# Second expert layer of a two-layer decoder: ScalarE zeroes the accumulator, VectorE ends a tile ahead of the next bias, and batch 0 is normalised in the stage ahead

## The reference, cut to what matters

```python
x = hidden_states.reshape(-1, H)                       # 1024 tokens, H = 256
expert_idx = argmax(softmax(x @ Wr.T), -1)             # 8 experts
inter = zeros((1024, 1024))
for e in range(8):
    mask = (expert_idx == e)[:, None]
    inter = inter + mask * gelu(x @ W1[e] + b1[e])     # W1[e]: 256 x 1024
y = inter @ Wo + bo + x
out = (y - mean) * rsqrt(var + 1e-12) * gamma + beta   # added to the stream by the caller
```

## Time and profile before

| what | us |
| --- | --- |
| median of 3 runs (lowest, highest) | 1063.65 (1060.42, 1067.02) |
| the profiled execution, device time | 1065.01 |
| its span, first to last instruction | 1063.2 |
| second expert stage in the span | 914.4 to 1063.2 |
| PE busy over the span | 916.1 (86%) |
| DVE, ACT, POOL busy | 649.7 (61%), 461.4 (43%), 329.7 (31%) |
| mean granted TensorE clock | 0.937 |

### The profile page before, as it was taken

The page is one execution under the profiler, slowest core; times in us unless marked ns, Lnnn a source line. Parts: engine busy times, 40 slices in busy tenths (PEclk is TensorE's granted clock), DMA queues, the critical chain, the costliest instruction groups (busy, mean ns, idle before and its releaser), DMA issues. The chain is left out here.

```text
span 1063.2 us, 12776 instructions
## 1 busy us (share of the span) xinstructions
PE 916.1 (86%) x4044; PEld 465.7 (44%) x4044; DVE 649.7 (61%) x1329; ACT 461.4 (43%) x918; POOL 329.7 (31%) x336
## 2 busy tenths in 40 slices
PE   5878878999999964999799999997779997559975
PEld 2435534333332234567455555553323333434554
DVE  5856558888889534454165556544679994446443
ACT  3786444777777721121243333322128774013320
POOL 7226535200000001464074555541300000335514
PEclk9989999999999995999899999998979999659998
DMA  4040053033228208232930000001100100463000
GB/s 145 1 149 0 1 102 57 1 46 46 48 62 254 94 1 305 78 119 88 356 131 1 1 1 1 0 1 53 33 1 30 33 1 1 155 235 92 11 10 30
DMA packets 41653, 73.77 MB, mean 69 GB/s; under 512 B 8964, under 2 KB 27780, under 8 KB 40436
## 3 DMA queue, kind: packets, MB, share of 16 engines
q1 hardware_dynamic: 36228, 59.42, 18.6%
q0 software_dynamic: 4400, 13.11, 3.8%
q10 hardware_dynamic: 960, 0.43, 0.2%
HBM read 49.67 MB, written 10.49 MB: 57 GB/s over the span
## 5 line engine op out<-in xcount | busy, mean ns | idle before, releaser
L1063 DVE TENSOR_REDUCE c_amx<-PS 128x1 f32<-128x512 f32 x256 | 158.7, 682 | 29.8 <-PE PS L963 29.6
L1155 ACT ACTIVATE c_aE<-PS 128x512 f32<-128x512 f32 x256 | 132.5, 603 | 47.1 <-PE PS L975 46.9
L1764 POOL TENSOR_SCALAR s_Pn<-s_Pr,s_rs 128x512 f32<-128x512 f32 x64 | 99.9, 1563 | 108.2 <-DVE s_rs L1790 108.1
L68 POOL TENSOR_SCALAR rstd<-mv 128x4 f32<-128x4 f32 x8 | 1.9, 233 | 342.0 <-DVE mv L91 342.0
L963 PE MATMUL PS<-c_aKs,c_aQs 99*128 99x512 bf16 x256 | 95.1, 383 | 7.4 <-DMA c_aQs<-area 3.9
L975 PE MATMUL PS<-c_aQs,c_aKs 99*128 99x512 bf16 x256 | 94.5, 380 | 3.5 <-ACT c_aE L1155 2.3
L1848 ACT ACTIVATE s_Pr<-PS,s_nmx 128x512 f32<-128x512 f32 x64 | 44.0, 688 | 116.2 <-DVE s_nmx L1783 116.2
L1781 DVE TENSOR_REDUCE s_mx<-PS 128x1 f32<-128x512 f32 x64 | 44.2, 690 | 69.0 <-PE PS L1895 69.0
L1063 DVE TENSOR_REDUCE h_amx<-PS 128x1 f32<-128x512 f32 x128 | 79.7, 682 | 7.8 <-PE PS L963 7.5
L1155 ACT ACTIVATE h_aE<-PS 128x512 f32<-128x512 f32 x128 | 67.9, 601 | 23.6 <-PE PS L975 23.2
L986 PE MATMUL PS<-c_aE,c_VB 128*17 128x512 f32 x512 | 67.4, 598 | 0.1
(11 more groups left out here) (426 smaller groups left out, 1731.7 us busy)
## 6 DMA issues: line engine op xcount, KB each, us to landing
area<-in_e_w SPq DMA_DIRECT2D x16, 512.0 KB, 9.1
area<-in_g_w SPq DMA_DIRECT2D x8, 1024.0 KB, 15.9
c_aKs<-area SPq DMA_DIRECT2D x48, 128.0 KB
g_B<-in_g_b SPq DMA_DIRECT2D x1, 4096.0 KB, 15.8
c_aQs<-area SPq DMA_DIRECT2D x48, 64.0 KB
h_aQs<-h_QP SPq DMA_DIRECT2D x48, 64.0 KB
early<-in_ctxT SPq DMA_DIRECT2D x2, 1024.0 KB, 8.8
e_B<-in_e_b SPq DMA_DIRECT2D x1, 2048.0 KB, 11.4
```

The source lines that it names most:

```text
L1063: dve.tensor_reduce(self.mx[:, qt, j, half:half + 1], PS[:, n % MB, :], AX.X, ALU.max).then_inc(self.max_done, 1)
L1155: act.activation(self.E[kt % 2][:, j, :], PS[:, MB + x % XB, :], ACT.Exp, scale=0.25).then_inc(self.exp_done, 1)
L1764: pool.tensor_scalar(Pn[g % NPB][:, :], Pr[g % NPB][:, :], rs[:, g % NPB:g % NPB + 1], None, ALU.mult).then_inc(pn_ready, 1)
```

## The change

- `OutputProjection.vector` normalises the 4 tiles of batch 0 in its second call (b = 1), between the copies to XT and the additions of batch 1, after a wait for the first `rstd`. `normalise_vector`, `Norm` and `transposes_tensor` take a `first` and leave batch 0 out. This holds for both cross stages, so both expert stages begin with batch 1 alone, and TensorE transposes batch 0 with no wait.
- The router's matmuls wait for XT by batch. `SlotInverse.vector` makes V ahead of R, and the second expert stage reads the sources ahead of three more operations.
- In the second expert stage ScalarE zeroes `Hall`, by 8 activations with scale 0 that read the identity matrix. SyncE's transfers are in another order, under one semaphore each for what waits for them: the normalised rows first, then B1, the rows for the residual, W2, gamma and beta, B2.
- VectorE's loop runs `hidden(p+1)`, `add_hidden(p)` for p = 0 to 9. Then it waits for `rest_ready` and for each tile runs `add_hidden`, `residual(t)`, `finish(t)`, `hidden`. GpSimd scatters tile t right after its deviation. `down(7)` writes bank 0, and doesn't wait for `residual(6)`.
- The last stage doesn't clear its semaphores (`release` in place of `clear`).

```diff
+        if b == 1:
+            dve.wait_ge(self.following.rstd_ready, 1)
+            for i in range(TB):
+                dve.tensor_scalar(sh.XN[:, i, :], sh.X[:, i, :], sh.mv[:, i, 0:1], sh.rstd[:, i:i + 1],
+                                  ALU.subtract, ALU.mult).then_inc(self.first_normed, 1)
...
             self.following.tile(dve, i, self.out_taken, i + 1)
+        if b == 1:
+            dve.wait_ge(self.first_normed, TB)
...
+        c.link(dve.tensor_tensor(self.TH[:, :, :], self.tile1[:, :].unsqueeze(2).to_broadcast(wide),
+                                 self.iota.unsqueeze(1).to_broadcast(wide), ALU.is_equal))
+        dve.tensor_scalar(self.V[:, :, 0, :], self.TH[:, :, :], self.rowid, None, ALU.mult).then_inc(self.V_ready, 1)
+        dve.tensor_tensor(self.V[:, :, 1, :], self.TH[:, :, :], self.next_tile.unsqueeze(2).to_broadcast(wide),
+                          ALU.mult).then_inc(self.V_ready, 1)
...
             for i in range(NT):
+                pe.wait_ge(nm.xT_ready, KD * (i // TB + 1))
...
-            for d, s in ((wr, "g_wr"), (iota, "iota")):
-                sp.dma_start(d[tuple(slice(None) for _ in d.shape)], A[s]).then_inc(small_in, 16)
+            sp.dma_start(wr[:, :, :], A["g_wr"]).then_inc(wr_in, 16)
             sp.dma_start(inv.const[:, :], A["inv_const"]).then_inc(const_in, 16)
+            sp.dma_start(iota[:, :], A["iota"]).then_inc(iota_in, 16)
+            for b in range(B):
+                i = slice(b * TB, (b + 1) * TB)
+                nm.stored(sp, b)
+                sp.dma_start(xn_rows.rearrange("(t p) c -> p t c", p=P)[:, i, :], XN[:, i, :]).then_inc(xn_stored, 16)
+            sp.dma_start(B1[:, :], A["g_b1"].to_broadcast([P, EXP * F])).then_inc(b1_in, 16)
             whole = rows.rearrange("(t p) c -> p t c", p=P)
             sp.dma_start(whole[:, :, D:2 * D], X[:, :, :]).then_inc(rows_stored, 16)
-            for b in range(B):
-                i = slice(b * TB, (b + 1) * TB)
-                sp.wait_ge(nm.xn_ready, b + 1)
-                sp.dma_start(xn_rows.rearrange("(t p) c -> p t c", p=P)[:, i, :], XN[:, i, :]).then_inc(xn_stored, 16)
             sp.dma_start(whole[:, :, 0:D], XN[:, :, :]).then_inc(rows_stored, 16)
-            sp.dma_start(B1[:, :], A["g_b1"].to_broadcast([P, EXP * F])).then_inc(b_in, 16)
-            sp.dma_start(B2[:, :], A["g_b2"]).then_inc(b_in, 16)
             sp.dma_start(W2[:, :, :], A["g_w2"]).then_inc(w2_in, 16)
+            sp.dma_start(gb[:, :, :], A["g_gb"]).then_inc(rest_in, 16)
+            sp.dma_start(B2[:, :], A["g_b2"]).then_inc(rest_in, 16)
...
-            for i in range(NT):
-                last = pool.memset(Hall[:, i * F:(i + 1) * F], 0.0)
-            last.then_inc(hall_zero, 1)
...
                 inverse_deviation(t)
-                if t > 0:
-                    put_out(t - 1)
-            put_out(NT - 1)
+                put_out(t)
...
+            inv.vector_sources(dve, c)
             c.link(dve.tensor_tensor(turn[:, :], turn[:, :], iota[:, 0:EXP], ALU.add))
             c.link(dve.tensor_tensor(passed[:, :, 0:EXP - 1],
                                      turn[:, 0:EXP - 1].unsqueeze(1).to_broadcast([P, 16, EXP - 1]),
                                      iota[:, :].unsqueeze(2).to_broadcast([P, 16, EXP - 1]), ALU.is_lt))
             c.link(dve.tensor_reduce(exf[:, :], passed[:, :, 0:EXP - 1], AX.X, ALU.add))
-            inv.vector_sources(dve, c)
...
             hidden(0)
-            for p in range(NT + LAG + 2):
+            dve.wait_ge(hall_zero, NT)
+            for p in range(LAG + 1):
+                hidden(p + 1)
+                add_hidden(p)
+            dve.wait_ge(rest_in, 32)
+            dve.wait_ge(rest_ready, 1)
+            for t in range(NT):
+                p = LAG + 1 + t
+                if p < PAIRS:
+                    add_hidden(p)
+                residual(t)
+                finish(t)
                 if p + 1 < PAIRS:
                     hidden(p + 1)
-                if p == 0:
-                    dve.wait_ge(hall_zero, 1)
-                if p < PAIRS:
-                    add_hidden(p)
-                t = p - LAG - 1
-                if t == 0:
-                    dve.wait_ge(rest_ready, 1)
-                if 0 <= t < NT:
-                    residual(t)
-                if 0 <= t - 1 < NT:
-                    finish(t - 1)
...
+            for i in range(NT):
+                act.activation(Hall[:, i * F:(i + 1) * F].rearrange("p (k n) -> p k n", k=KF),
+                               sh.ident[:, :].unsqueeze(1).to_broadcast([P, KF, P]), ACT.Copy,
+                               scale=0.0).then_inc(hall_zero, 1)
...
             def down(t):
                 pe.wait_ge(hT_ready, t + 1)
-                if t > 0:
+                if 0 < t < NT - 1:
                     pe.wait_ge(z_ready, t)
+                elif t == NT - 1:
+                    pe.wait_ge(xsT_ready, PAIRS)
                 else:
                     pe.wait_ge(ids_ready, 1)
+                    pe.wait_ge(w2_in, 16)
                 for k in range(KF):
-                    last = pe.matmul(PS[:, 7, 0:D], HT[t % 2][:, k, :], W2[:, k, :],
+                    last = pe.matmul(PS[:, down_bank(t), 0:D], HT[t % 2][:, k, :], W2[:, k, :],
                                      start=(k == 0), stop=(k == KF - 1))
                 last.then_inc(w2_mm, 1)
 
             transpose_x(0)
...
             s(nc, own := StageSemaphores(nc), sh, A)
-            own.clear()
+            if n + 1 < len(stages):
+                own.clear()
+            else:
+                own.release()
```

More of the change, by code:

```diff
@@ L49, in layernorm_vector, with normalise_vector @@
     normalise_vector(dve, src, dst, mv, rstd, rstd_ready, normed)
-def normalise_vector(dve, src, dst, mv, rstd, rstd_ready, normed):
-    for b in range(B):
+def normalise_vector(dve, src, dst, mv, rstd, rstd_ready, normed, first=0):
+    for b in range(first, B):
         if rstd_ready is not None:
@@ L96, in gpsimd, with transposes_tensor @@
                                   self.var_ready, self.eps_added, self.rstd_ready)
-def transposes_tensor(pe, PS, XN, ident, ready, per_batch, done, loaded=None):
+def transposes_tensor(pe, PS, XN, ident, ready, per_batch, done, loaded=None, first=0):
     for b in range(B):
-        if loaded is None:
-            pe.wait_ge(ready, (b + 1) * per_batch)
-        else:
+        if loaded is not None:
             pe.wait_ge(loaded[b], 16)
+        elif b >= first:
+            pe.wait_ge(ready, (b + 1 - first) * per_batch)
         for k in range(KD):
@@ L1178, in __init__ @@
         self.at, self.sh, self.w, self.w_in, self.w_loads = at, sh, w, w_in, w_loads
-        self.o_placed, self.oT_done, self.oT_ready, self.out_mm, self.out_taken = (
-            sem("po_" + n) for n in ("o_placed", "oT_done", "oT_ready", "out_mm", "out_taken"))
+        self.o_placed, self.oT_done, self.oT_ready, self.out_mm, self.out_taken, self.first_normed = (
+            sem("po_" + n) for n in ("o_placed", "oT_done", "oT_ready", "out_mm", "out_taken", "first_normed"))
     @staticmethod
@@ L1234, in vector, with __init__ @@
             self.following.tile(dve, i, self.out_taken, i + 1)
+        if b == 1:
+            dve.wait_ge(self.first_normed, TB)
 class Norm:
-    def __init__(self, nc, ctx, sh, name):
-        self.sh, self.xn_loaded = sh, None
+    def __init__(self, nc, ctx, sh, name, first=0):
+        self.sh, self.xn_loaded, self.first = sh, None, first
         self.xn_ready, self.xT_done, self.xT_ready = (
@@ L1246, in vector, with stored @@
     def vector(self, dve):
-        normalise_vector(dve, self.sh.X, self.sh.XN, self.sh.mv, self.sh.rstd, None, self.xn_ready)
+        normalise_vector(dve, self.sh.X, self.sh.XN, self.sh.mv, self.sh.rstd, None, self.xn_ready,
+                         self.first)
+    def stored(self, eng, b):
+        if b >= self.first:
+            eng.wait_ge(self.xn_ready, b + 1 - self.first)
     def tensor(self, pe):
-        transposes_tensor(pe, self.sh.PS, self.sh.XN, self.sh.ident, self.xn_ready, 1, self.xT_done, self.xn_loaded)
+        transposes_tensor(pe, self.sh.PS, self.sh.XN, self.sh.ident, self.xn_ready, 1, self.xT_done, self.xn_loaded,
+                          self.first)
     def scalar(self, act):
@@ L2729, in experts1_stage @@
     out_rows = sh.out.rearrange("p i d -> (p i) d")
-    small_in, b_in, w2_in, ones_set, hall_zero = (
-        sem(n) for n in ("small_in", "b_in", "w2_in", "ones_set", "hall_zero"))
+    wr_in, iota_in, b1_in, w2_in, rest_in, ones_set, hall_zero = (
+        sem(n) for n in ("wr_in", "iota_in", "b1_in", "w2_in", "rest_in", "ones_set", "hall_zero"))
     own, lg_mm, oh_ready, rank_mm, ext_ready, trib_made, const_in = (
@@ L2744, in experts1_stage, with down_bank @@
     rstd_ready, scaled, out_ready = (sem(n) for n in ("rstd_ready", "scaled", "out_ready"))
-    NSMALL = 3
+    def down_bank(t):
+        return 7 if t < NT - 1 else 0
```

(9 more changed lines are left out.)

29 lines of the change are left out of this document (10 added, 19 removed).

## The result

The changed kernel takes 1047.58 us (median of 4 runs, 1047.17 to 1052.45); the kernel before took 1062.95 in the 4 runs it is compared with. The ratio is 0.9861, 95% interval [0.9828, 0.9895]: faster by 1.4%, where 22 us or 2.1% were forecast. The profiled execution took 1047.17 us (span 1045.3), 17.8 less than that of before.

What follows compares the result with a forecast made beforehand. TensorE was held by VectorE's norm alternating with GpSimd's memsets and by VectorE's late read of PSUM bank 7. Terms 7.4 + 2.1 + 0.8 - 0.3 + 9.5 + 1.0 + 1.5 = 22.0 took 1063.65 to 1041.7 us, range 1034.5 to 1049.

Steps and rivals of the forecast that it cites:

- gains given back: Rival: half clock stays (1.7), gathers come 3 us late, barriers' time stays; 5.7 less gained, 1047.4 us; chance 0.16.
- Start of the second expert stage: Norm, transposes and router there: TensorE transposes at once without a break, 10.65 and 0.15 against 18.25; 7.4 us less.
- Start of the first: First expert stage's norm, transposes and router: 10.8 us in place of 12.86; 2.1 us less.
- Routing: Second expert stage, VectorE with V ahead of R: only two operations stand ahead of the product's read; 0.8 us less.
- The first gather: Second expert stage: issued 8.2 us earlier, sharing DMA engines with SyncE's last transfers; 0.3 us more, bounds nothing and 8.2.
- The pair loop: Second expert stage: first gap stays, later gaps (7.2) and half clock (1.7) go, ending at 1042.5 against 1052.09; 9.5 less.
- Last scatter: Kernel's end: it no longer follows tile 6's scatter on GpSimd; 1.0 us less.
- Barriers: Behind the block at the program's end: they go, 1.5 us less, between 0 and 1.5.
- The clock is released early: Rival: unbroken TensorE work brings clock 1.00, router's matmuls take 3.5 for 7.0 in both expert stages; 1034.7 us; chance 0.12.
- No effect: Rival: memsets didn't hold the norm back, batch 1 still takes 4 x 1.06; 1044.1 us, part of the forecast's 0.63.
- loop keeps its gaps: Rival: another wait replaces bank 7's in the pair loop; 7.2 less gained, with half clock 8.9, 1050.6 us; chance 0.04.
- the slower rival: VectorE's round in the pair loop becomes the bound; at 10 us more from GpSimd's deviation, 1077.7 us; chance 0.02.

Runs made afterwards that it cites:

- e10: The changed kernel with batch 0's norm back in the expert stages, zeroing still on ScalarE: 1048.47 us, ratio 0.9834 to the kernel before.
- e1: The changed kernel with SyncE issuing g_rows, W2, gb and B2 only once the first gather has landed: 1046.09 us, ratio 0.9822 to before.
- e3: The changed kernel with GpSimd's additions told tile by tile and VectorE waiting for its own tile alone: 1045.30 us, ratio 0.9818 to before.
- e8: The changed kernel with the barriers that clear the last stage's semaphores back at the program's end: 1049.38 us, ratio 0.9890 to before.
- e6: The kernel before with one part of the change, ScalarE zeroing the accumulator in place of GpSimd: 1060.98 us, ratio 0.9975 to before.
- e11: The changed kernel with g_rows issued in 16 transfers of one tile in place of two: 1047.26 us, ratio 0.9842 to before.
- e2: The changed kernel with W2, gb and B2 waiting for the first gather, g_rows still ahead of it: 1047.36 us, ratio 0.9842 to before.
- e4: The changed kernel with VectorE's and GpSimd's order in the pair loop as it was before: 1054.25 us, ratio 0.9888 to before.
- e5: The changed kernel with the accumulator zeroed by 8 memsets on GpSimd again: 1050.75 us, ratio 0.9890 to before.

## Why the prediction was right, and where it wasn't

Direction and range were right: 1047.58 lies in 1034.5 to 1049, at its upper end. So was the mechanism of every term but one; by its own signs the prediction was wrong there ("if the gathers land in 5 us or more": the first was used 7.4 us after its issue). The time is that of the rival *gains given back* (1047.4). By the terms of the sum, profile against profile:

- Start of the second expert stage: 7.4 forecast, 18.24 - 10.26 = 8.0 measured. Start of the first: 2.1 forecast, 12.86 - 10.06 = 2.8. e10 shows 1.44 of each to be the norm that moved.
- Routing: 0.8 forecast; the gather's issue came 8.75 earlier, less the 8.0 is 0.75.
- **The first gather: 0.3 forecast, 4.4 measured. This is the step that failed.** I chose "nearest to the low end" because the gather of before was fast at the edge of full DMA engines. But the earlier trace rows showed one issued when SyncE's queue was all but empty, and that says nothing on one issued 5 us before it is. e1 took the queued transfers away and had 3.1 us. What the forecast lacked is the pause: beside a full SyncE queue the gather's first packet comes 3.1 to 3.5 us after its issue, not 0.7.
- **The pair loop: 9.5 forecast, 107.2 - 99.7 = 7.5 measured** from the first use of a gather to the last matmul. Of the 2.0 missing 1.5 are the half clock behind the first gap, that I "count as gone" (5.12 us against 3.62). The sentence was wrong by its own rows: the first gap stayed, and the half clock had followed that one alone. e3 shows that it goes with the gap. The other 0.5 lies ahead of `down(1)`, which was forecast 0.3 us later than before, counted from the first gather's use, and came 1.0 later (58.96 against 57.98): from GpSimd's last addition to it are 2.7 us in place of 1.9, since VectorE needs 0.9 us from that addition to the start of its own. (The 0.2 us for the restart stand in the forecast twice; that changes nothing here.)
- Last scatter 1.0: measured 4.30 - 3.27 = 1.0. Barriers 1.5: measured 1.4, and e8 brings back 1.5.

Sum: 2.8 + 8.0 + 0.75 - 4.4 + 7.5 + 1.0 + 1.4 = 17.05. The other 0.8 of the profiles' difference lies ahead of the second expert stage and was not traced: up to the first expert stage the changed kernel is 2.0 later, from there to the second 5.7 less, of which 2.8 are counted. The medians differ by 15.4, since the profiled run of before was 2.1 over its median and that of the changed kernel 0.4 under its own.

Of the rivals: *gains given back* had three losses; two came (3 forecast and 4.4 measured, 1.7 and 1.5), the barriers' didn't. That the number fits it to 0.2 us is in part luck: by the profiles 17.8 us were gained, by the medians 15.4. *The clock is released early* didn't come in the changed kernel's own profile (6.83 us at 0.50 in both stages). But in the twelve profiles with other edits the second stage's router took 3.9 to 4.7 us in seven, and the first stage's 4.0 and 4.9 in two (e10, e6). The rows brought against it were of one execution, and don't exclude it. *No effect* is refuted by L58's pitch, *loop keeps its gaps* by the rows. VectorE's round never became the bound, and the stage had none of the slower rival.

## What to carry to other kernels

When a step is brought forward, look at what its DMA queue neighbours are doing at the new time, not at the old: a gather that was fast behind a burst of transfers is slow inside it, here by 4.4 of the 8.7 us that it was issued earlier. Holding the transfers back gave the 3 us again (e1); cutting them into 16 gave 1.3 of the some 4 us (e11 beside e8). A wait for a whole set of results, where a consumer needs the first, is worth telling piece by piece, and on TensorE the gap costs its half clock as well (3.6 + 1.5 us here). And parts of 1 to 3 us are to be judged in the profile, from a fixed event on, where single runs differ by 1% and more; there too the clock's state has to be noted beside each row.

## What the runs showed of the hardware

- A first gather of 128 rows is used 3.0 to 3.1 us after its issue with SyncE's queue empty, and 5.5 to 7.7 us beside SyncE's queued transfers. The DMA share ahead of the issue doesn't tell which: it was 0.99 before the fast gather of the earlier trace rows and 0.95 before the slow one.
- The pause ahead of that gather's first packet was 3.1 to 3.5 us beside a full SyncE queue, with g_rows in 2 transfers or in 16.
- Behind a gap of 2.46 to 3.58 us at the same place TensorE ran the next 16 matmuls in 5.1 to 6.7 us in place of 3.62, in all ten profiles with that gap (before, changed, and e1, e2, e4, e5, e6, e8, e10, e11). But in e4 gaps of 1.95 to 2.17 us, and in e6 and the kernel before one of 2.52 us, were followed by 3.69. What else the clock looks at was not found.
- The router's 32 matmuls behind 16 transposes, 10.3 us without a break, ran at 0.50 throughout in the changed kernel; in e8, the same up to there, they took 4.00 us.
- By the Trainium skill, SBUF — State Buffer, Who interferes with whom, a VectorE instruction with two SBUF inputs and a GpSimd instruction that reads SBUF contend. The trace agrees. In e3 GpSimd's addition takes 0.71 us alone and 1.7 where it meets VectorE's addition to Hall:

```profile
984.34 0.72 POOL L2818 TENSOR_TENSOR X<-X,g_gb 128x256 f32<-128x256 f32 x1
985.72 1.72 POOL L2818 TENSOR_TENSOR X<-X,g_gb 128x256 f32<-128x256 f32 x1
```
```profile
985.59 1.27 DVE L2924 SCALAR_TENSOR_TENSOR g_Hall<-g_H,g_inside,g_Hall 128x1024 f32 x1
```
